# Attention with a gated expert layer, 16 batches on one core: when the projection matrix and the value bias are prepared, which engine subtracts the input's low half, and how a pair's second unit is scored

## The chip, the cores and the metric

One core of one Trainium2 chip. The metric is the device time of one launch in microseconds (us). The kernel before took 1359.69 us, the median of three runs (1359.64 to 1359.70).

## The reference

For each of 16 batches of 512 tokens with 128 features (all float32):

```
xn  = layernorm(x)                                  # no gain, no bias
q,k,v = xn @ Wq^T + bq, xn @ Wk^T + bk, xn @ Wv^T + bv   # 16 heads of 64
att = softmax(mask(q k^T / 8)) / 8                  # causal
a   = reshape(att @ v) @ proj                       # proj: 1024 x 128
g   = one-hot(argmax) * softmax(l2norm(xn Wp^T + bp) @ l2norm(sim) * exp(min(temp, ...)))   # 4 experts
f   = xn @ W^T + sum_e g_e * (xn Wd_e^T) Wu_e^T     # ranks 1, 2, 4, 8
out = x + a + f
```

The attention result is reshaped from (head, token, 64) without a transposition: each head fills 32 of the 512 rows.

## The kernel before, in words

**Precision.** Large products are made of three matmuls on fp32r operands, each operand being a high part (a rounded copy) and a low part (the rest): high by high, high by low, low by high. Where the contraction is over 64 elements only, two of the three are put on one matmul over 128 partitions: `q_parts` holds a head's high and low query halves, `k_twice` its high keys twice. A second matmul adds the low keys, `k_low`, whose other 64 rows are zero (L1246).

**Units and steps.** A batch is 8 pairs of heads (`NPAIR`), a pair is 4 units (`NBLK`): unit i scores 128 queries against its first 128(i+1) keys. A batch has 32 steps, one unit each (s = 4p + i). In step s the tensor engine scores unit s, both heads (`score`, L1227), transposes the probabilities of unit s-3 (`transpose`, L1248), runs the job of the step if `JOBS` has one (a q, k or v projection, the input's transposition `xt` in step 25, the router in step 1, the gated values in step 17), the value product of a pair every fourth step, and quarters of the output projection. Each engine has this order written out by hand in its own `step`, and the engines meet at semaphores only. Step numbers stand in constants at the top (`STEP_...`).

**Who does what.** For unit s the vector engine (DVE) takes the masked maximum out of PSUM (`maximum`, L934), the scalar engine (ACT) the exponentials with their sums (L693), DVE the reciprocals (L932), GpSimd (POOL) the multiplication by them (`normalise`, L601, the instruction is L608). ACT evacuates the transposed probabilities of head 0 (L704), DVE those of head 1 (L955). For a q or k job ACT makes the high half, DVE the low half, POOL pads the low keys (L568), and SyncE (SP) copies the halves into `q_parts` and `k_twice` by DMA (L438 to L448). For `xt` (step 25, `FIRST_X`) ACT makes `xt`, `xq_hi`, `xt_hi`, and DVE subtracts `xq_lo` (L823) and `xt_lo` (L839). In DVE's step the order is: maximum of head 0, maximum of head 1, `router_early` (L976), then `follow()` (reciprocals and the evacuation L955), `router_late` (L1000), jobs and statistics. In the last unit of a pair `follow()` stands between the two maxima.

**PSUM.** Two banks `scores`. A pair's first unit (i = 0) has both heads in bank 0: one matmul of `q_hi` against the low keys of both heads (L1222), then one per head (L1225). Units 1 to 3 have head h in bank h, two matmuls per head (L1243, L1246). `place` tells DVE where a head lies. Before unit 1 the tensor engine waits for both maxima of unit 0 (L1242).

**First batch.** Setup is mixed into its first steps. SP loads `projs`, the 1024 x 128 projection matrix, into a corner of `pt` (L482). POOL splits it into `proj_hi` and `proj_lo` after `normalise` of step 1 (L597, L599). DVE makes the three parts of the experts' up matrices in step 1 (`experts_up`, L900) and the value bias in step 3 (`value_bias`, L919), for which the tensor engine has made, after step 2, one transposition and eight float32 matmuls `bvt` by `projs` (L1210, L1214). They are first used in step 24 (`lora`, L1305) and by `project` (L1291).

**End.** After the last step the tensor engine makes, in this order: transposition of unit -3, values of pair -2, transposition of unit -2, the last two quarters of half the projection, transposition of unit -1, values of pair -1, and the rest.

Of the kernel before, what the change touches and what calls it, by code (L numbers as in the profile page):

```python
# [40 lines left out]
P = 128  # L41
# [164 lines left out]
def place(s, h):  # L206


    return (0, P * h) if s % NBLK == 0 else (h, 0)


def build(nc, x, Wq, bq, Wk, bk, Wv, bv, proj, W, Wp, bp, sim, temp, Wd, Wu, out):
    with ExitStack() as ctx:
# [79 lines left out]
        w_in = [pt[:, n // 2, n % 2, 0:2, :].rearrange("p a (c e) -> p (a c) e", e=E) for n in range(3)]  # L293
        projs = pt[:, 1, 1, 0:2, :].rearrange("p a (c e) -> p (a c) e", e=E)
        bv_rows = pt[:, 1, 1, 2, 0:P]
# [3 lines left out]
        z_lo = sb("z_lo", [P, 2, NPAIR, OCT, ROWS], F32R)  # L299
        y_t = sb("y_t", [P, S])  # L300


# [15 lines left out]
        proj_loaded = sem("proj_loaded")  # L318
        proj_split = sem("proj_split")
        bv_loaded = sem("bv_loaded")  # L320
        heads_marked = sem("heads_marked")
# [79 lines left out]
        def _(sp):  # L401
# [79 lines left out]
            sp.wait_ge(qk_moved[0], setup.moved(NPAIR))  # L481
            sp.dma_start(projs, proj.rearrange("(c p) e -> p c e", p=P)).then_inc(proj_loaded, 16)  # L482
            for s in MOVED_STEPS:
# [14 lines left out]
        def _(pool):  # L498
# [95 lines left out]

            def projection_parts():
                pool.wait_ge(proj_loaded, 16)
                nc.gpsimd.tensor_copy(proj_hi[:], projs).then_inc(proj_split, 1)  # L597
                pool.wait_ge(proj_split, 1)
                nc.gpsimd.tensor_tensor(proj_lo[:], projs, proj_hi[:].bitcast(F32), ALU.subtract)\  # L599
                    .then_inc(proj_split, 1)  # L600

# [8 lines left out]
            def batch(b, last):  # L610
                c = Counts(pool, b)
                for s in range(UNITS):
# [21 lines left out]
                    if b == 0 and s == 1:  # L634
                        projection_parts()
                    if s == STEP_RSTD and not last:
# [155 lines left out]
        def _(dve):  # L792
# [20 lines left out]

            def job(c, s, back=0):
                kind, n = JOBS[s]
# [4 lines left out]
                if kind == "xt":  # L820
                    dve.wait_ge(xt_ready, c.at(1, 2))
                    dve.wait_ge(xq_hi_ready, c.at(1, 2))
                    nc.vector.tensor_tensor(by_parity(xq_lo[:]), evens_first(xt[:]),  # L823
                                            by_parity(xq_hi[:].bitcast(F32)), ALU.subtract).then_inc(xq_lo_ready, 1)
                if kind in HI_KINDS:
# [35 lines left out]
            done.then_inc(xn_ready, 1)  # L861

# [17 lines left out]
            nc.vector.tensor_copy(bqk[:], jobp[0][:, 0:2 * NPAIR]).then_inc(bqk_ready, 1)  # L880
            job(before, FIRST_X)
            weights(1)
# [36 lines left out]
            def value_bias():  # L919

                dve.wait_ge(proj_split, 2)
                dve.wait_ge(bias_bank_ready, 1)
                nc.vector.tensor_copy(wut[0:GATED, :], outp[0:GATED, 2 * P:3 * P]).then_inc(small_ready, 1)
                dve.wait_ge(heads_marked, 4)
                link(nc.vector.tensor_copy(bias_hi[GATED:P, :], outp[GATED:P, 0:E]))
                link(nc.vector.scalar_tensor_tensor(
                    out=wut[GATED:P, :], in0=bias_hi[GATED:P, :].bitcast(F32), scalar=late_rows[GATED:P, 0:1],
                    in1=outp[GATED:P, 0:E], op0=ALU.mult, op1=ALU.add))

# [45 lines left out]
            def router_early(c, s):  # L975


                if s == STEP_SUMS:

                    dve.wait_ge(products_ready, c.at(1, 1))  # L980
                    nc.vector.tensor_reduce(unorm[:, 0, :], usq[:], AX_X, ALU.add).then_inc(unorm_ready, 1)
                    nc.vector.tensor_reduce(lg[:, 0, :, :], uprod[:], AX_X, ALU.add).then_inc(r_chain, 1)
                if s == STEP_LOGITS:

# [8 lines left out]
                        .then_inc(lg_ready, 1)  # L993
                if s == STEP_FIRST:

                    dve.wait_ge(r_chain, c.at(R_CHAIN, 9))
                    nc.vector.tensor_reduce(row[:, 4, :], ranked, AX_X, ALU.max).then_inc(r_chain, 1)
                    dve.wait_ge(r_chain, c.at(R_CHAIN, 10))
                    nc.vector.tensor_tensor(top, ranked, over_experts(row[:, 4, :]), ALU.is_ge).then_inc(r_chain, 1)

            def router_late(c, s):


                if s == STEP_WEIGHTS:
# [66 lines left out]
            def batch(b, first, last):  # L1071
                c = Counts(dve, b)
                for s in range(UNITS):
# [4 lines left out]
                    if first and s == 1:  # L1078
                        weights(4)
                        experts_up()  # L1080
                        weights(5)
                    if first and s == 2:
                        similar_units()
                    if first and s == 3:
                        value_bias()
# [15 lines left out]
            reciprocals(c, -1)  # L1101
            evacuate_pt(c, -3)
            low_z(c, -2)
            evacuate_pt(c, -2)
            evacuate_pt(c, -1)
# [6 lines left out]
        def _(pe):  # L1112
# [53 lines left out]
            weights(0)  # L1166
            pe.wait_ge(xn_ready, 1)
            for i in range(NBLK):
                done = nc.tensor.transpose(scores[0][:, P * i:P * i + P], xn[:, i, :], ident[:])
            done.then_inc(job_ready[bank_of(FIRST_X)], 1)  # L1170
# [36 lines left out]
            def value_bias():  # L1207
# [3 lines left out]
                                    up_parts[:].rearrange("p a b -> p (a b)").bitcast(F32), ident[:])  # L1211
                pe.wait_ge(proj_loaded, 16)
# [4 lines left out]
            def first_scores(c, s):  # L1217


                p = s // NBLK  # L1220
                wait(pe, sm_ready, c.head(s - 1, 0))
                nc.tensor.matmul(scores[0][:, 0:2 * P].rearrange("p (h k) -> p h k", k=P), q_hi[:, p % 2, 0:P],  # L1222
                                 k_low[:, :, p % 2, 0:P], start=True, stop=False, skip_group_check=True)
                for h in range(2):
                    nc.tensor.matmul(scores[0][:, P * h:P * h + P], q_parts[:, h, p % 2, 0:P],  # L1225
                                     k_twice[:, h, p % 2, 0:P], start=False, stop=True,
                                     skip_group_check=True).then_inc(s_ready, 1)  # L1227

            def score(c, s, first):
                i, p = s % NBLK, s // NBLK  # L1230
                if i == 0:
# [4 lines left out]
                    pe.wait_ge(low_padded, c.values(p, 1))  # L1236
                    first_scores(c, s)
# [46 lines left out]
            def project(c, o, quarter):  # L1284

                pe.wait_ge(z_ready, c.pair(OCT_PAIRS * (o + 1) - 1))
                pe.wait_ge(proj_split, 2)
                cols = OCT * ROWS * (o % NOCT)
# [30 lines left out]
            def step(c, s, first=False, last=False, tail=False):  # L1319
# [29 lines left out]
            def batch(b, first, last):  # L1349
                c = Counts(pe, b)  # L1350
                for s in range(UNITS):
                    step(c, s, first, last)
                    if first and s == 1:
                        weights(5)
                    if first and s == 2:
                        value_bias()
# [63 lines left out]
```

## Time and profile before

| | |
|---|---|
| median of 3 runs | 1359.69 us |
| the profiled execution | 1360.15 us |
| its span | 1358.4 us |
| TensorE busy (matmul) | 1340.1 us, 99% of the span, 10925 matmuls |
| VectorE, ScalarE, GpSimd busy | 1102.7, 1088.4, 969.3 us |
| granted TensorE clock | 1.00 |

Busy time is the union of an engine's instructions. A matmul's record starts when it is issued and its end is modelled, so neighbouring records overlap; the distance between two starts tells how fast TensorE goes. "Idle before" is the time that the engine had nothing running before the instruction, with what ended it. L608 is line 608 of the kernel. In the timeline, instructions of one group are merged into one row with their count.

### The profile page before, as it was taken

The page shows a single profiled execution, that of the slowest core. Times are in us where ns is not written, and L with a number is a line of the kernel's source. Part 1 is how long each engine was busy: PE and PEld are TensorE (multiplying, and loading weights), DVE is VectorE, ACT ScalarE, POOL GpSimd, SP SyncE. Part 2 cuts the span into 40 slices and gives each one's busy share as a digit, 9 for nine tenths or more (in the row PEclk, how much of TensorE's full clock was granted, in tenths as well). Part 3 has the DMA queues.
Part 4 walks back from the last instruction along what each step waited for, and adds up shares of the span by engine and source line. Part 5 has one row for each costly group of instructions (what it writes and reads, how often), then busy time and mean ns, then how long its engine had stood idle before and what let it go on. Part 6 is the DMA issues. An engine that isn't in the chain of part 4 may idle for free. (4 is left out here: it accounts for less than half of the span.)

```text
span 1358.4 us, 34725 instructions
## 1 busy us (share of the span) xinstructions
PE 1340.1 (99%) x10925; PEld 1139.4 (84%) x10925; DVE 1102.7 (81%) x4015; ACT 1088.4 (80%) x3161; POOL 969.3 (71%) x1421
## 2 busy tenths in 40 slices
PE   6999999999999999999999999999999999999998
PEld 5788888888888888888888888888888888888887
DVE  7978878788787887878788787887878878788785
ACT  5888888878878887887878788788888887888785
POOL 6777776777766776767777667777677776677664
PEclk9999999999999999999999999999999999999999
DMA  5544444544445455444544444454454454445441
GB/s 138 117 102 113 116 116 97 124 113 105 118 106 129 95 118 124 103 112 114 118 102 113 117 108 111 112 122 110 100 122 114 103 122 113 118 97 120 113 102 48
DMA packets 112690, 150.87 MB, mean 111 GB/s; under 512 B 18239, under 2 KB 47230, under 8 KB 112510
## 3 DMA queue, kind: packets, MB, share of 16 engines
q1 hardware_dynamic: 111646, 148.36, 46.1%
q8 instruction: 91, 1.49, 0.5%
q14 instruction: 89, 0.73, 0.2%
q10 hardware_dynamic: 864, 0.29, 0.1%
HBM read 10.69 MB, written 4.19 MB: 11 GB/s over the span
## 5 line engine op out<-in xcount | busy, mean ns | idle before, releaser
L608 POOL TENSOR_TENSOR prob<-prob,rden 128x128 f32<-128x128 f32 (+3 forms) x1024 | 712.3, 720 | 292.8 <-DVE rden L932 286.6
L943 DVE CUSTOM_DVE_ANT_0 prob<-scores,mask 128x128 f32<-128x128 f32 (+3 forms) x1024 | 470.5, 487 | 210.7 <-issue 148.6
L693 ACT ACTIVATE prob<-prob,nmax 128x128 f32<-128x128 f32 (+3 forms) x1024 | 567.8, 560 | 14.0 <-DVE nmax L943 6.2
L1255 PE MATMUL ptp<-ident,prob 128*128 128x128 f32 x2560 | 370.0, 274 | 1.1 <-POOL prob L608 0.6
L1255 PEld LDWEIGHTS ptp<-ident,prob 128*128 128x128 f32 x2560 | 296.0, 141 | 30.2 <-issue 8.5
L1279 PE MATMUL zp<-pt,v_sb 128*64 128x64 f32 (+3 forms) x4096 | 307.7, 303 | 1.0 <-DVE z_lo L961 0.8
L704 ACT ACTIVATE pt<-ptp 128x128 f32<-128x128 f32 (+3 forms) x512 | 221.3, 432 | 105.5 <-PE ptp L1255 105.5
L1243 PE MATMUL scores<-k_twice,q_parts 128*128 128x256 f32 (+2 forms) x768 | 267.8, 356 | 3.1 <-DVE nmax L943 3.1
L1279 PEld LDWEIGHTS zp<-pt,v_sb 128*64 128x64 f32 x4096 | 221.6, 137 | 52.3 <-issue 14.8
L1246 PE MATMUL scores<-k_low,q_parts 128*128 128x256 f32 (+2 forms) x768 | 254.1, 338 | 0.0
L955 DVE COPY pt<-ptp 128x128 f32<-128x128 f32 (+3 forms) x512 | 243.0, 475 | 2.0 <-PE ptp L1255 1.3
L568 POOL CAST k_low<-k_lo 64x512 fp32r<-64x512 f32 x256 | 155.7, 608 | 73.7 <-DVE k_lo L831 63.2
L1243 PEld LDWEIGHTS scores<-k_twice,q_parts 128*128 128x128 f32 x768 | 144.0, 187 | 67.0 <-issue 42.7
L693 ACT ACTIVATION_READ_ACCUMULATOR prob<-prob,nmax 128x1 f32 x1024 | 198.3, 194 | 0.0
L682 ACT ACTIVATE z_hi<-zp 128x512 fp32r<-128x512 f32 x128 | 76.6, 598 | 133.2 <-PE zp L1279 131.5
L1246 PEld LDWEIGHTS scores<-k_low,q_parts 128*128 128x128 f32 x768 | 144.8, 188 | 15.2
L835 DVE SCALAR_TENSOR_TENSOR q_lo<-jobp,bqk,q_hi 128x512 fp32r<-128x512 f32 x128 | 95.2, 744 | 2.4 <-ACT q_hi L674 1.5
L831 DVE SCALAR_TENSOR_TENSOR k_lo<-jobp,bqk,k_hi 128x512 fp32r<-128x512 f32 x128 | 95.1, 743 | 0.5 <-ACT k_hi L671 0.5
L961 DVE TENSOR_TENSOR z_lo<-zp,z_hi 128x512 fp32r<-128x512 f32 x128 | 87.8, 686 | 2.5 <-ACT z_hi L682 2.5
L671 ACT ACTIVATE k_hi<-jobp,bqk 128x512 fp32r<-128x512 f32 x128 | 86.7, 677 | 0.5 <-PE jobp L1192 0.5
L674 ACT ACTIVATE q_hi<-jobp,bqk 128x512 fp32r<-128x512 f32 x128 | 85.8, 670 | 0.7 <-PE jobp L1182 0.7
L943 DVE DVE_READ_ACCUMULATOR2_ANT nmax<- 128x1 f32 x1024 | 85.1, 83 | 0.2
(183 smaller groups left out, 1829.7 us busy)
## 6 DMA issues: line engine op xcount, KB each, us to landing
k_twice<-k_hi SPq DMA_DIRECT2D x508, 128.0 KB, 2.3
q_parts<-q_lo SPq DMA_DIRECT2D x256, 128.0 KB, 2.5
q_parts<-q_hi SPq DMA_DIRECT2D x254, 128.0 KB, 2.3
xin<-in_L_attn_x_dram SPq DMA_DIRECT2D x16, 256.0 KB, 3.8
xres<-in_L_attn_x_dram SPq DMA_DIRECT2D x16, 256.0 KB, 3.1
out_dram<-osb SPq DMA_DIRECT2D x15, 256.0 KB, 2.6
pt<-in_L_attn_Wq_dram SPq DMA_DIRECT2D x1, 512.0 KB, 4.8
pt<-in_L_attn_Wk_dram SPq DMA_DIRECT2D x1, 512.0 KB, 6.8
```

What stands on the lines that cost most here:

```text
L568: nc.gpsimd.tensor_copy(k_low[own(h), h, n % 2, :], k_lo[own(h), :].bitcast(F32))\
L608: nc.gpsimd.tensor_tensor(part, part, scale, ALU.mult).then_inc(pn_ready, 1)
L693: nc.scalar.activation(part, part, ACT.Exp, bias=nmax[:, s % NROT, h:h + 1], scale=-1.0, accum_out=den[:, s % NROT, h:h + 1]).then_inc(p_r ...
L704: nc.scalar.activation(pt[:, p % 2, 0, 0:i + 1, P * i:P * i + P], src, ACT.Copy)\
L831: done = nc.vector.scalar_tensor_tensor(out=k_lo[:], in0=src[:], scalar=bqk[:, NPAIR + n:NPAIR + n + 1], in1=k_hi[:].bitcast(F32), op0=ALU ...
L835: done = nc.vector.scalar_tensor_tensor(out=q_lo[:, n % 2, :], in0=src[:], scalar=bqk[:, n:n + 1], in1=q_hi[:, n % 2, :].bitcast(F32), op0 ...
L943: nc.vector.tensor_tensor_reduce(out=prob[:, s % NROT, h, 0:cols], in0=scores[bank][:, first_col:first_col + cols], in1=mask[:, S - cols:S ...
L955: nc.vector.tensor_copy(pt[:, p % 2, 1, 0:i + 1, P * i:P * i + P], src).then_inc(pt_ready[1], 1)
L1243: nc.tensor.matmul(scores[h][:, 0:width(s)], q_parts[:, h, p % 2, queries], k_twice[:, h, p % 2, 0:width(s)], start=True, stop=False)
L1246: nc.tensor.matmul(scores[h][:, 0:width(s)], q_parts[:, h, p % 2, queries], k_low[:, h, p % 2, 0:width(s)], start=False, stop=True).then_i ...
L1255: done = nc.tensor.transpose(ptp[h][:, P * j:P * j + P], prob[:, s % NROT, h, P * j:P * j + P], ident[:])
L1279: done = nc.tensor.matmul(zp[DH * odd:DH * odd + DH, z0 + P // 2 * j:z0 + S // 2], v_sb[:, j, col:col + DH], seen, start=j == NBLK - 1, st ...
```

## The change

1. A pair's second unit (i = 1) is scored like the first: one bank (bank 1) holds both heads, one matmul of `q_hi` against both heads' low keys (512 columns), then one of 256 columns per head. `maximum` waits for both heads there. The waits for free banks follow: unit 1 waits for the last maximum of the unit two before it, unit 2 head 0 for unit 0, head 1 for unit 1.
2. `xt_lo` is subtracted by POOL (`low_inputs`, at the head of step 25, before `normalise`) in all batches; only the setup's own stays on DVE.
3. `proj` is loaded in two halves into `y_t` and `osb`. POOL splits them in steps 6 and 10 of the first batch, and in step 14 adds up its eight 128 x 128 chunks in three additions; the value bias is then one matmul in place of eight. The tensor engine does this after step 18, DVE `experts_up` in step 13 and `value_bias` in step 21.
4. The router's logits (step 6) come behind the reciprocals and the evacuation L955 in DVE's step (`router_late`), no longer ahead of them.
5. In the setup each normalised block of `xn` is signalled by itself, so its transposition can start.
6. At the end the tensor engine transposes unit -1 ahead of the two projection quarters, and DVE evacuates unit -2 ahead of `low_z`.

```
 def place(s, h):
-    return (0, P * h) if s % NBLK == 0 else (h, 0)
+    return (s % NBLK, width(s) * h) if s % NBLK < 2 else (h, 0)
...
+STEP_SPLIT, STEP_SUMMED, STEP_UP, STEP_BIAS_BANK, STEP_BIAS = (6, 10), 14, 13, 18, 21
...
+            def projection_parts(half):
+                chunks = slice(NBLK * half, NBLK * half + NBLK)
+                pool.wait_ge(proj_loaded, 32)
+                nc.gpsimd.tensor_copy(proj_hi[:, chunks, :], proj_in[half]).then_inc(proj_split, 1)
+                pool.wait_ge(proj_split, 2 * half + 1)
+                nc.gpsimd.tensor_tensor(proj_lo[:, chunks, :], proj_in[half], proj_hi[:, chunks, :].bitcast(F32),
+                                        ALU.subtract).then_inc(proj_split, 1)
+            def projection_sum():
+                pool.wait_ge(proj_split, 4)
+                nc.gpsimd.tensor_tensor(proj_in[0], proj_in[0], proj_in[1], ALU.add).then_inc(proj_summed, 1)
+                for n, cols in enumerate((2 * E, E)):
+                    pool.wait_ge(proj_summed, n + 1)
+                    nc.gpsimd.tensor_tensor(y_t[:, 0:cols], y_t[:, 0:cols], y_t[:, cols:2 * cols], ALU.add)\
+                        .then_inc(proj_summed, 1)
+            def low_inputs(c):
+                made = c.fixed(c.hi(FIRST_X))
+                pool.wait_ge(job_hi[bank_of(FIRST_X)], made)
+                nc.gpsimd.tensor_tensor(xt_lo[:], xt[:], xt_hi[:].bitcast(F32), ALU.subtract)\
+                    .then_inc(job_done[bank_of(FIRST_X)], 1)
...
+                    if s == FIRST_X and not last:
+                        low_inputs(c)
                     normalise(c, s)
...
-                scored, turned = c.fixed(c.head(s, 1 if s % NBLK == 0 else h)), c.fixed(c.head(s - NROT, h))
+                scored, turned = c.fixed(c.head(s, 1 if s % NBLK < 2 else h)), c.fixed(c.head(s - NROT, h))
...
-                for n in range(NPAIR):
-                    done = nc.tensor.matmul(outp[:, 0:E], bvt[:], projs[:, n, :], start=n == 0, stop=n == NPAIR - 1)
-                done.then_inc(bias_bank_ready, 1)
+                pe.wait_ge(proj_summed, 3)
+                nc.tensor.matmul(outp[:, 0:E], bvt[:], y_t[:, 0:E], start=True, stop=True).then_inc(bias_bank_ready, 1)
+            def narrow_scores(c, s):
+                i, p = s % NBLK, s // NBLK
+                cols, queries = width(s), slice(P * i, P * i + P)
+                wait(pe, sm_ready, c.head(s - 1, 0) if i == 0 else c.head(s - 2, 1))
+                nc.tensor.matmul(scores[i][:, 0:2 * cols].rearrange("p (h k) -> p h k", k=cols), q_hi[:, p % 2, queries],
+                                 k_low[:, :, p % 2, 0:cols], start=True, stop=False, skip_group_check=True)
                 for h in range(2):
+                    nc.tensor.matmul(scores[i][:, cols * h:cols * h + cols], q_parts[:, h, p % 2, queries],
+                                     k_twice[:, h, p % 2, 0:cols], start=False, stop=True,
                                      skip_group_check=True).then_inc(s_ready, 1)
...
-                    wait(pe, sm_ready, c.head(s - 1, 1 if i == 1 else h))
+                    wait(pe, sm_ready, c.head(s - 1, h) if i == 3 else c.head(s - 2 + h, 1))
...
+                if first and s == STEP_BASE:
+                    pe.wait_ge(wut_ready, 2)
...
             transpose(c, -2)
+            transpose(c, -1)
             project(c, -2, 2)
             project(c, -2, 3)
-            transpose(c, -1)
```

## Rows read from the trace of the kernel before

**Rows 1.** Source view of L1138, the input's transposition, four matmuls in each batch

```profile
L1138 PE MATMUL jobp<-ident,xn x60: 272/273/273, 82.4 to 1243.8; 128*128 128x128 f32 x60
```

**Rows 2.** Stretches: length, then busy time of PE, PEld, DVE, ACT, POOL

```profile
622.00:664.00 42.00, 42.00 (x348) 36.11 (x346) 35.38 (x131) 33.97 (x102) 30.64 (x45) 1.00 0.48 111
```

**Rows 3.** Timeline of TensorE, first batch: start, length, line, [idle before <- releaser]

```profile
9.60 1.12 PE L1161 MATMUL outp<-ident,pt 128*128 128x128 f32 x4 [0.44 <-DMA pt<-in_L_attn_Wk_dram]
...
24.62 1.95 PE L1214 MATMUL outp<-pt,bvt 128*128 128x128 f32 x16
...
32.49 0.39 PE L1243 MATMUL scores<-k_twice,q_parts 128*128 128x256 f32 x1 [2.36 <-DVE nmax L943]
```

**Rows 4.** Timeline of TensorE's weight loads at 28.4 us

```profile
28.42 0.19 PEld L1222 LDWEIGHTS scores<-k_low,q_hi 128*128 128x128 f32 x1 [0.44 <-DMA k_twice<-k_hi]
```

**Rows 5.** Timeline of VectorE, first batch

```profile
23.93 0.48 DVE L906 TENSOR_TENSOR up_parts<-small_in,up_parts 128x32 fp32r<-128x32 f32 x1
...
30.89 0.29 DVE L923 CAST wut<-outp 96x128 fp32r<-96x128 f32 x1 [1.91 <-POOL proj_lo L599]
...
31.93 0.29 DVE L943 CUSTOM_DVE_ANT_0 prob<-scores,mask 128x128 f32<-128x128 f32 x1
```

**Rows 6.** Timeline of GpSimd, first batch

```profile
27.37 1.03 POOL L597 CAST proj_hi<-pt 128x1024 fp32r<-128x1024 f32 x1
28.48 2.37 POOL L599 TENSOR_TENSOR proj_lo<-pt,proj_hi 128x1024 fp32r<-128x1024 f32 x1
30.81 1.61 POOL L608 TENSOR_TENSOR prob<-prob,rden 128x384 f32<-128x384 f32 x2
```

**Rows 7.** Timeline of TensorE: transpositions of a 128-key unit in steps 3, 7 and 27

```profile
606.93 0.38 PE L1255 MATMUL ptp<-ident,prob 128*128 128x128 f32 x2
...
616.86 0.51 PE L1255 MATMUL ptp<-ident,prob 128*128 128x128 f32 x2
...
668.29 0.48 PE L1255 MATMUL ptp<-ident,prob 128*128 128x128 f32 x2
```

**Rows 8.** Timeline of VectorE ahead of the stall in step 7

```profile
615.27 0.32 DVE L987 TENSOR_TENSOR lg<-lg,unorm 128x16 f32<-128x16 f32 x1
...
616.25 0.67 DVE L955 COPY pt<-ptp 128x512 f32<-128x512 f32 x1
```

**Rows 9.** Timeline of VectorE ahead of the stall in step 27

```profile
665.18 0.91 DVE L823 TENSOR_TENSOR xq_lo<-xt,xq_hi 128x512 fp32r<-128x512 f32 x1 [1.04 <-ACT xq_hi L668]
666.02 0.68 DVE L839 TENSOR_TENSOR xt_lo<-xt,xt_hi 128x512 fp32r<-128x512 f32 x1
...
667.65 0.67 DVE L955 COPY pt<-ptp 128x512 f32<-128x512 f32 x1
```

**Rows 10.** Timeline of ScalarE, then of GpSimd, around step 25

```profile
664.95 0.62 ACT L669 ACTIVATE xt_hi<-jobp 128x512 fp32r<-128x512 f32 x1
...
667.88 2.84 POOL L608 TENSOR_TENSOR prob<-prob,rden 128x256 f32<-128x256 f32 x4 [2.32 <-DVE rden L932]
```

**Rows 11.** Timeline of TensorE: starts of 512-column and of 256-column matmuls

```profile
606.00 0.39 PE L1243 MATMUL scores<-k_twice,q_parts 128*128 128x512 f32 x1
606.23 0.40 PE L1246 MATMUL scores<-k_low,q_parts 128*128 128x512 f32 x1
...
610.00 0.28 PE L1243 MATMUL scores<-k_twice,q_parts 128*128 128x256 f32 x1
610.12 0.28 PE L1246 MATMUL scores<-k_low,q_parts 128*128 128x256 f32 x1
```

**Rows 12.** Groups of instructions, VectorE from 100 to 1300 us: count | busy, mean | idle before

```profile
L943 DVE CUSTOM_DVE_ANT_0 prob<-scores,mask 128x384 f32<-128x384 f32 x232 | 120.1, 554 | 120.6 <-issue 110.4 <-PE scores L1246 10.2
```

**Rows 13.** Waits, 100 to 1300 us: who <- for whom: total us, times, longest

```profile
PEld scores L1243 <- DVE nmax L943: 3.8, 18, 0.3
```

**Rows 14.** Timeline of TensorE at the end

```profile
1334.10 0.39 PE L1243 MATMUL scores<-k_twice,q_parts 128*128 128x256 f32 x1 [0.77 <-DVE nmax L943]
...
1348.52 2.40 PE L1279 MATMUL zp<-pt,v_sb 128*64 128x64 f32 x32 [0.25 <-ACT pt L704]
```

More of the change, by code:

```diff
@@ L319, in build @@
         proj_split = sem("proj_split")
+        proj_summed = sem("proj_summed")
+        wut_ready = sem("wut_ready")
+        xn_block = sem("xn_block")
         bv_loaded = sem("bv_loaded")
@@ L481, in _ @@
             sp.wait_ge(qk_moved[0], setup.moved(NPAIR))
-            sp.dma_start(projs, proj.rearrange("(c p) e -> p c e", p=P)).then_inc(proj_loaded, 16)
+            for half in range(2):
+                sp.dma_start(proj_in[half], proj.rearrange("(c p) e -> p c e", p=P)[:, NBLK * half:NBLK * half + NBLK, :])\
+                    .then_inc(proj_loaded, 16)
             for s in MOVED_STEPS:
@@ L633, in batch @@
                         pad_low_keys(c, s)
-                    if b == 0 and s == 1:
-                        projection_parts()
+                    if b == 0 and s in STEP_SPLIT:
+                        projection_parts(STEP_SPLIT.index(s))
+                    if b == 0 and s == STEP_SUMMED:
+                        projection_sum()
                     if s == STEP_RSTD and not last:
@@ L812, in variances, with job @@
                 nc.vector.tensor_tensor(var_eps[:], meanvar[:, :, 1], eps[:], ALU.add).then_inc(var_ready, 1)
-            def job(c, s, back=0):
+            def job(c, s, back=0, setup=False):
                 kind, n = JOBS[s]
@@ L824, in job @@
                                             by_parity(xq_hi[:].bitcast(F32)), ALU.subtract).then_inc(xq_lo_ready, 1)
+                    if not setup:
+                        return
                 if kind in HI_KINDS:
@@ L860, in _ @@
                                                ALU.subtract, ALU.mult)
-            done.then_inc(xn_ready, 1)
+                done.then_inc(xn_block if n < NBLK - 1 else xn_ready, 1)
             links = [0]
@@ L880, in _ @@
             nc.vector.tensor_copy(bqk[:], jobp[0][:, 0:2 * NPAIR]).then_inc(bqk_ready, 1)
-            job(before, FIRST_X)
+            job(before, FIRST_X, setup=True)
             weights(1)
@@ L982, in router_early, with router_late @@
                     nc.vector.tensor_reduce(lg[:, 0, :, :], uprod[:], AX_X, ALU.add).then_inc(r_chain, 1)
+                if s == STEP_FIRST:
+                    dve.wait_ge(r_chain, c.at(R_CHAIN, 9))
+                    nc.vector.tensor_reduce(row[:, 4, :], ranked, AX_X, ALU.max).then_inc(r_chain, 1)
+                    dve.wait_ge(r_chain, c.at(R_CHAIN, 10))
+                    nc.vector.tensor_tensor(top, ranked, over_experts(row[:, 4, :]), ALU.is_ge).then_inc(r_chain, 1)
+            def router_late(c, s):
                 if s == STEP_LOGITS:
@@ L993, in router_early @@
                         .then_inc(lg_ready, 1)
[L994 to L1001, printed above, removed]
                 if s == STEP_WEIGHTS:
@@ L1083, in batch @@
                         similar_units()
-                    if first and s == 3:
+                    if first and s == STEP_UP:
+                        experts_up()
+                    if first and s == STEP_BIAS:
                         value_bias()
@@ L1166, in _ @@
             weights(0)
-            pe.wait_ge(xn_ready, 1)
             for i in range(NBLK):
+                pe.wait_ge(xn_block, min(i + 1, NBLK - 1))
+                if i == NBLK - 1:
+                    pe.wait_ge(xn_ready, 1)
                 done = nc.tensor.transpose(scores[0][:, P * i:P * i + P], xn[:, i, :], ident[:])
@@ L1211, in value_bias @@
                                     up_parts[:].rearrange("p a b -> p (a b)").bitcast(F32), ident[:])
-                pe.wait_ge(proj_loaded, 16)
-                for n in range(NPAIR):
-                    done = nc.tensor.matmul(outp[:, 0:E], bvt[:], projs[:, n, :], start=n == 0, stop=n == NPAIR - 1)
-                done.then_inc(bias_bank_ready, 1)
[L1217 to L1223, printed above, removed]
+                pe.wait_ge(proj_summed, 3)
[6 more added lines that the diff above has]
+                                 k_low[:, :, p % 2, 0:cols], start=True, stop=False, skip_group_check=True)
                 for h in range(2):
-                    nc.tensor.matmul(scores[0][:, P * h:P * h + P], q_parts[:, h, p % 2, 0:P],
-                                     k_twice[:, h, p % 2, 0:P], start=False, stop=True,
+                    nc.tensor.matmul(scores[i][:, cols * h:cols * h + cols], q_parts[:, h, p % 2, queries],
+                                     k_twice[:, h, p % 2, 0:cols], start=False, stop=True,
                                      skip_group_check=True).then_inc(s_ready, 1)
@@ L1236, in score @@
                     pe.wait_ge(low_padded, c.values(p, 1))
-                    first_scores(c, s)
+                if i < 2:
+                    narrow_scores(c, s)
                     return
@@ L1354, in batch @@
                         weights(5)
-                    if first and s == 2:
+                    if first and s == STEP_BIAS_BANK:
                         value_bias()
```

20 lines of the change are left out of this document (6 added, 14 removed).

## The prediction

> **What bounds the kernel now.** The page comes first: TensorE has something running in 99% of the span, the next engine in 81%. Then the period: the input's transposition comes once per batch, first at 82.4 us and for the fifteenth time at 1243.8 us [rows 1], so a batch takes 1161.4 / 14 = 82.96 us, and in a stretch of 42 us in mid-run TensorE is busy for all 42.00, the others for 30.6 to 35.4 [rows 2]. From about 40 us on time is TensorE's own work. But a busy row can hide a wait, since ends are modelled and overlap, so the timeline is read for places where the same work takes longer. Two recur in each batch. The two transpositions of a 128-key unit take 0.38 us in step 3, but 0.51 in step 7 and 0.48 in step 27 [rows 7]. I found the first in 14 of 15 batches after the first one, the second in all 15 batches that have an `xt` job. Both wait for the bank that DVE's evacuation L955 frees. Last come the first 40 us and the last 25, where TensorE really is idle [rows 3, 14]. The terms are made against the profiled execution (1360.15 us, span 1358.4 and 1.75 around it); the median lies 0.46 below, and I subtract the terms from the median.
>
> **Startup.** Before, DVE comes to `value_bias` in step 3 and waits 1.91 us for POOL's `proj_lo`; with its own three operations it gets to the maximum of unit 4 only at 31.93 [rows 5]. The score of unit 5 needs it, and TensorE stands still for 2.36 us [rows 3]. POOL has spent 27.37 to 30.81, 3.44 us, on the projection's parts, with `normalise` of unit 2 behind it [rows 6]. All this leaves. Score of unit 4 does not move: it waited for the copies into `k_twice`, to 28.42 [rows 4], and SP's queue of copies stays as it is (one more load, 512 KB in two pieces, issued well before). With some 0.65 us for its three matmuls, maximum 4 starts at about 29.1 instead of 31.93, 2.8 us earlier. Score of unit 5 no longer waits for it at all, only for unit 3. POOL's unit 2 stood behind POOL's own 3.44 us only; with them gone it comes up to 3.4 us earlier, and I take 3.2, to 27.6, since its reciprocals are then the next thing late. In the timeline POOL has no gap from there to unit 8, so step by step TensorE's transpositions follow it. I take 3.1 us at step 8, bounds 2.0 (the copies for unit 8 come with only part of the shift) and 3.6 (2.36 of wait and the 1.95 us of small matmuls, less what the copies hold at 28.42). TensorE must still make the value bias, after step 18, where it is the bound: one transposition and one matmul, some 0.3 us, against the 1.95 us of before [rows 3]. Net 2.8 us.
> The moved steps need cover. `experts_up` (0.7 us, its longest operation 0.48 [rows 5]) goes to step 13, `value_bias` (1.04 us, 30.89 to 31.93) to step 21, both in a unit i = 1. Ahead of the maxima of the next unit DVE idles 120.6 us in 232, or 1.04 per unit [rows 12]; that hides them, and if it were gone they would cost 0.7 and 1.0 once. POOL's halves are 1.03 / 2 + 2.37 / 2 = 1.7 us each in steps 6 and 10 [rows 6], its sums about 2.1 (2.37 / 2 for 512 columns, half and a quarter of that for 256 and 128) in step 14. They stand in front of `normalise` of a 512-key unit, which the tensor engine wants three steps later, while POOL idles 11 us of 42 [rows 2]. Step 6 falls where POOL is late anyway: up to 1.7 us there is the lower bound's reason. Unmoved is the time to the first score: a transposition per block of `xn` ends up to 0.7 us earlier, but the next work waits for Wk's load (0.44 idle, to 9.60 [rows 3]), so 0.
>
> **Step 7.** DVE runs the logits' chain from 615.27 before the evacuation at 616.25 [rows 8]; behind it now, the evacuation starts about 0.8 us earlier and its 0.13 us of stall goes. The chain (0.9 us) ends in ACT's small exponential in step 7, in front of an evacuation: it gets its input 0.7 us later than before, which is just when ACT comes to it. 14 x 0.13 = 1.8 us; 0 if ACT becomes late.
>
> **Step 27.** DVE makes `xq_lo` and then `xt_lo` (0.68), two maxima and the late evacuation at 667.65 [rows 9]. Without `xt_lo` the maxima start when the scores allow, 0.3 us earlier or more; 0.10 is needed [rows 7]. 15 x 0.10 = 1.5 us. POOL takes it over: it has the high half at 665.57, and idles 2.32 us before 667.88 [rows 10]. Its own price is not in the trace for this form; the subtraction of twice the size took 2.37, so 1.2 us, at the earliest done at 666.8, where DVE was at 666.70. TensorE's next job on that bank comes after the transpositions of 668.29 [rows 7]. Hidden; with no cover it would cost 15 x 1.2 = 18 us.
> DVE reads two SBUF tensors in L823 to 666.09 [rows 9] just as POOL would begin. The Trainium skill (SBUF — State Buffer, "SBUF: two separate sides") says that such an operation and a GpSimd one hold a common port pair exclusively. By that rule POOL would start at 666.09 and end at 667.3, still before 667.88; no run here shows it for this pair yet.
>
> **Second unit in one bank.** Per pair, four matmuls of 256 columns become one of 512 and two of 256. Starts lie 0.23 us apart at 512 columns and 0.12 at 256 [rows 11], so nearly nothing is gained: between 0 and 0.01 us per pair. Over 128 pairs I take 0.4 us, bounds 0 and 1.3. The lost waits of scores for maxima are 3.8 us in 18 cases by weight loads, much of it hidden behind running matmuls [rows 13]: 0.4 us, bounds 0 and 0.8.
> The Trainium skill (TensorEngine Tiling, "Instruction Overhead") gives each matmul some 60 cycles of overhead, an estimate of 25 ns at 2.4 GHz and 3.2 us for 128 matmuls. The rows above speak against it.
>
> **End.** In the last batch the score of unit 29 waits 0.77 us for unit 28's maxima [rows 14]; now it waits for unit 27's. All behind it follows TensorE: 0.7 us. The new order of the tail: the transposition of unit -1 waits for unit -2's evacuation, then the projection waits for `low_z`, now behind that evacuation; by my count the last values start at about 1348.55, against 1348.52 with 0.25 us of idle before it [rows 14]. So 0, bounds -0.3 and +0.3.
>
> **Sum.** 2.8 + 1.8 + 1.5 + 0.4 + 0.4 + 0.7 = 7.6 us; 1359.69 - 7.6 = 1352.1 us. Its own range by the bounds is 1350.2 to 1354.3. A difference of 0.2%, 2.7 us, is about what a measurement can tell from none.
>
> **Rivals.** *The startup gain is held back* (0.11): POOL's 1.7 us in step 6 and again in step 10 land on transpositions. For it: no gap on POOL there; against: the unit behind each has three steps of slack. About 2 us lost: 1354.1. *The two stalls stay* (0.06), because ACT's small exponential or the scores themselves hold the evacuation: 3.3 us not won, 1355.4. *Fewer matmuls are worth more* (0.05): a matmul has a fixed part that my rounded starts hide. If each of 128 were worth a fifth of its 0.12 us slot, it would be 3.1 us, 2.7 more than taken: 1349.4; this is what the cited overhead rule would do. *Slower* (0.04): `maximum` of head 0 in the second unit now waits for the matmuls of both heads, two slots of 0.12 us later. DVE has 1.04 us of idle per unit right after [rows 12]. If the unit's chain through exponential and reciprocals sets TensorE's pace, 128 x 0.23 = 29 us come on top: 1381.5. It decides from the point at which that idle falls below 0.23. That the change does not do what it says is no case here: each of its parts is an instruction in another place.
>
> **Numbers.** The forecast has 0.74. The range 1350.0 to 1355.4 takes in the first two rivals. Faster by over 0.2% (below 1357.0): all but the slower rival and what the bounds leave: 0.93; within 0.2% 0.03; slower 0.04.
>
> **What the profile after should show.** 10783 matmul records in place of 10925 (one less in each of 128 pairs, and 2 for 16 in the bias); no TensorE idle at 30 to 32 us; unit 5's score near 30 us; batch period 82.96 - 0.25 = 82.7 us; the transpositions in steps 7 and 27 at 0.38 us; POOL's idle after step 25 shorter by 1.2 us; DVE's idle before second-unit maxima larger. I am wrong if the period is above 82.85, if a new wait of TensorE for POOL stands between 35 and 60 us, or if the first score moves.

## The result, and the profile after

The changed kernel took 1351.24 us, the median of six runs (1350.67 to 1351.71), against 1359.70 us for the kernel before beside it (1359.64 to 1359.84): the ratio is 0.9937 with a 95% interval of 0.9926 to 0.9949, some 8.5 us or 0.6% faster. The forecast was 1352.1, the range 1350.0 to 1355.4. Run again later as a yardstick it took 1351.36 against 1359.40.

The page of the kernel after, part 1, and the source view of the input's transposition [rows 1]:

```profile
PE 1330.2 (99%) x10783; PEld 1131.2 (84%) x10783; DVE 1106.4 (82%) x4000; ACT 1086.5 (81%) x3161; POOL 998.3 (74%) x1441
...
L1167 PE MATMUL jobp<-ident,xn x60: 272/273/273, 80.3 to 1234.9; 128*128 128x128 f32 x60
```

The span is 1348.9 us, the count of matmuls the 10783 that were forecast. Fourteen batches now take 1234.9 - 80.3 = 1154.6 us, before 1161.4 [rows 1]: 82.47 us each in place of 82.96, where I had forecast 82.7. So 6.8 us of the span's 9.5 lie in the steady part, 2.1 ahead of it (82.4 to 80.3), 0.6 behind. The forecast had split it otherwise: 4.1 steady, 2.8 at the start, 0.7 at the end. Of the 2.1, moreover, 0.9 lie before the first score, which stands at 17.22 instead of 18.14.

Timeline of TensorE, kernel after: step 7, then step 27 [rows 7], then the second unit of step 25 [rows 11]:

```profile
611.93 0.38 PE L1287 MATMUL ptp<-ident,prob 128*128 128x128 f32 x2
...
663.04 0.41 PE L1287 MATMUL ptp<-ident,prob 128*128 128x128 f32 x2
...
656.45 0.40 PE L1253 MATMUL scores<-k_low,q_hi 128*128 128x512 f32 x1
656.68 0.40 PE L1256 MATMUL scores<-k_twice,q_parts 128*128 128x256 f32 x2
656.92 0.38 PE L1287 MATMUL ptp<-ident,prob 128*128 128x128 f32 x2
```

The stall of step 7 is gone, that of step 27 all but 0.03 us of its 0.10. The second unit takes 656.92 - 656.45 = 0.47 us from its first start to the next work, as four matmuls of 0.12 us had taken 0.48.

Timeline around step 25, VectorE, then GpSimd [rows 9, 10]:

```profile
660.03 1.10 DVE L850 TENSOR_TENSOR xq_lo<-xt,xq_hi 128x512 fp32r<-128x512 f32 x1 [0.85 <-ACT xq_hi L695]
...
661.18 0.56 DVE L971 CUSTOM_DVE_ANT_0 prob<-scores,mask 128x384 f32<-128x384 f32 x1
```

```profile
659.31 1.28 POOL L574 CAST k_low<-k_lo 64x512 fp32r<-64x512 f32 x2 [0.41 <-DVE k_lo L860]
660.67 1.60 POOL L622 TENSOR_TENSOR xt_lo<-xt,xt_hi 128x512 fp32r<-128x512 f32 x1
662.38 1.19 POOL L631 TENSOR_TENSOR prob<-prob,rden 128x256 f32<-128x256 f32 x2
```

`xt_lo` fits: GpSimd's idle of 2.32 us is used up and `normalise` of unit 25 follows within 0.11 us. But `xq_lo` has grown from 0.91 to 1.10 us and `xt_lo` takes 1.60, not 1.2. It starts while `xq_lo` still runs and ends at 662.27, 1.14 us after `xq_lo`'s end at 661.13.

Timeline of the first batch, kernel after: TensorE, then VectorE, then GpSimd [rows 3 to 6]:

```profile
17.22 0.35 PE L1253 MATMUL scores<-k_low,q_hi 128*128 128x256 f32 x1
...
27.38 0.39 PE L1253 MATMUL scores<-k_low,q_hi 128*128 128x256 f32 x1 [1.25 <-DMA k_twice<-k_hi]
28.93 0.39 PE L1253 MATMUL scores<-k_low,q_hi 128*128 128x512 f32 x1
...
36.91 0.38 PE L1253 MATMUL scores<-k_low,q_hi 128*128 128x256 f32 x1 [1.32 <-DVE nmax L971]
...
54.68 0.50 PE L1275 MATMUL scores<-k_twice,q_parts 128*128 128x512 f32 x1 [0.25 <-DVE nmax L971]
```

```profile
50.81 1.08 DVE L1052 TENSOR_TENSOR gated<-dn,lg 128x128 f32<-128x128 f32 x1
...
53.57 0.58 DVE L935 TENSOR_TENSOR up_parts<-small_in,up_parts 128x32 fp32r<-128x32 f32 x1
54.07 0.54 DVE L971 CUSTOM_DVE_ANT_0 prob<-scores,mask 128x384 f32<-128x384 f32 x1
```

```profile
38.13 0.61 POOL L604 CAST proj_hi<-y_t 128x512 fp32r<-128x512 f32 x1
38.83 1.29 POOL L606 TENSOR_TENSOR proj_lo<-y_t,proj_hi 128x512 fp32r<-128x512 f32 x1
```

Unit 5 is scored at 28.93 instead of 32.49, with no wait; the forecast was near 30. About 1.0 of these 3.6 us is not won by the missing wait: unit 4 itself stands at 27.38 instead of 28.42, the first score being earlier. And TensorE then waits in places where it had not, or less. At the score of unit 8 (36.91) the matmul's row names the maximum of unit 7, but VectorE was done with that at 35.99; the weight load beside it waited 1.76 us for the copies into `k_twice` (0.41 before). In step 15 it waits for a maximum that VectorE reaches late, having the router's gated values (one operation of 1.08 us) and the up matrices in the same step 13.

End of the kernel after, TensorE [rows 14]:

```profile
1323.77 0.48 PE L1253 MATMUL scores<-k_low,q_hi 128*128 128x512 f32 x1
1324.09 0.40 PE L1256 MATMUL scores<-k_twice,q_parts 128*128 128x256 f32 x2
1324.96 0.41 PE L1287 MATMUL ptp<-ident,prob 128*128 128x128 f32 x2 [0.48 <-ACT pt L731]
```

The 0.77 us wait before unit 29's score is gone, but 0.48 us of it comes back one piece of work later, as a wait for ScalarE's evacuation.

### The profile page after: what moved, and what is told of

It is laid out like the page before. It is cut to its first block, busy times and chain, and to the rows that moved or that the text cites. A ratio compares the mean times of both kernels' runs of the same rounds, so it can differ in the third digit from the quotient of the medians.

```text
span 1348.9 us, 34446 instructions
## 1 busy us (share of the span) xinstructions
PE 1330.2 (99%) x10783; PEld 1131.2 (84%) x10783; DVE 1106.4 (82%) x4000; ACT 1086.5 (81%) x3161; POOL 998.3 (74%) x1441
## 4 chain that ended last, share of the span: by engine, by line
PE 95%; ACT 1%; DVE 0%; issue 0%
PE zp L1311 22%; PE ptp L1287 20%; PE jobp L1157 13%; PE scores L1275 9%; PE scores L1278 7%; PE outp L1323 7%; PE jobp L1162 6%; PE scores L1256 4%; PE scores L1253 3%; PE jobp L1172 1%; PE outp L1332 1%; ACT prob L720 1%; PE jobp L1177 1%; PE jobp L1348 0%; PE jobp L1167 0%; PE outp L1337 0%
## 5 line engine op out<-in xcount | busy, mean ns | idle before, releaser
L1275 PE MATMUL scores<-k_twice,q_parts 128*128 128x384 f32 (+1 forms) x512 | 201.3, 393 | 0.8 <-DVE nmax L971 0.8
L1278 PE MATMUL scores<-k_low,q_parts 128*128 128x384 f32 (+1 forms) x512 | 186.8, 365 | 0.0
L1275 PEld LDWEIGHTS scores<-k_twice,q_parts 128*128 128x128 f32 x512 | 95.9, 187 | 55.5 <-issue 42.7
L1278 PEld LDWEIGHTS scores<-k_low,q_parts 128*128 128x128 f32 x512 | 96.4, 188 | 9.7
L1256 PEld LDWEIGHTS scores<-k_twice,q_parts 128*128 128x128 f32 x512 | 87.5, 188 | 12.4
L1256 PE MATMUL scores<-k_twice,q_parts 128*128 128x128 f32 (+1 forms) x512 | 93.2, 263 | 0.0
L1253 PE MATMUL scores<-k_low,q_hi 128*128 128x256 f32 (+1 forms) x256 | 87.3, 341 | 2.6 <-DVE nmax L971 1.3
```

The source lines that it names most:

```text
L1256: nc.tensor.matmul(scores[i][:, cols * h:cols * h + cols], q_parts[:, h, p % 2, queries], k_twice[:, h, p % 2, 0:cols], start=False, stop= ...
```

## The experiments

Medians are set against the kernel before in the same runs. Each part of the change was put alone into the kernel before, then two of them together, then parts were taken out of or moved in the changed kernel.

**The second unit alone** (`b_narrow`: `place`, `narrow_scores` and the waits)

```
-    return (0, P * h) if s % NBLK == 0 else (h, 0)
+    return (s % NBLK, width(s) * h) if s % NBLK < 2 else (h, 0)
...
-            def first_scores(c, s):
+            def narrow_scores(c, s):
```

> The kernel before with the second unit's scoring alone (one bank, one shared low-key matmul, the new waits). From the trace of the changed kernel, where each second unit's scoring and the start behind it take 11 to 13 ns less: 128 x 0.012 = 1.5 us, and 0.3 to 0.7 us at the end where unit 29 no longer waits. Theory: 1.5 to 2.5 us faster than before. Fixed-overhead rival (25 ns per matmul left out): 3.2 us and the end's part, so 3.5 to 4 us faster. Rival of the late maximum: up to 29 us slower.

1359.59 us against 1359.49, ratio 1.0003 (0.9994 to 1.0011): no gain at all; neither the theory nor either rival said so. In its trace the steps with a second unit are each about 0.01 us shorter and unit 29's wait is gone, but step 26 has grown from 1.64 to 1.83 us in every batch.

**The logits later, alone** (`b_late`)

```
+            def router_late(c, s):
...
                 if s == STEP_LOGITS:
...
-            def router_late(c, s):
...
                 if s == STEP_WEIGHTS:
```

The head of `router_late` moves up, so that it takes in the block of the logits and runs it behind `follow()`.

> The kernel before with the router's logits behind the evacuation alone. Theory: the step-7 transpositions go from 0.51 to 0.38 us in every batch after the first, 15 x 0.12 = 1.8 us faster, and nothing else moves; step 27 stays at 0.48. Rival (ScalarE's exponential becomes late): no gain, a new wait of ScalarE before its evacuation in step 7.

1358.05 against 1359.49, ratio 0.9991 (0.9982 to 1.0000); its eleven runs, 1357.84 to 1358.73, all lie below all 33 of before, 1359.16 to 1359.84. So 1.4 us. Step 7 and step 27 of this kernel, TensorE's timeline, and ScalarE in step 7:

```profile
615.68 0.38 PE L1255 MATMUL ptp<-ident,prob 128*128 128x128 f32 x2
...
667.01 0.48 PE L1255 MATMUL ptp<-ident,prob 128*128 128x128 f32 x2
```

```profile
616.00 0.21 ACT L749 ACTIVATE lg<-lg 128x16 f32<-128x16 f32 x1
616.10 0.27 ACT L704 ACTIVATE pt<-ptp 128x128 f32<-128x128 f32 x1
```

The stall of step 7 goes and that of step 27 stays. ScalarE's exponential shows no wait before it: that rival falls.

**The low half by GpSimd, alone** (`b_low`)

```
+                    if s == FIRST_X and not last:
+                        low_inputs(c)
                     normalise(c, s)
...
+                    if not setup:
+                        return
```

> The kernel before with the input's low half by GpSimd alone. Theory: steps 26 and 27 lose 0.17 us per batch, 15 x 0.17 = 2.6 us faster; step 7 stays at 0.51. GpSimd's subtraction takes 1.6 us and VectorE's xq_lo goes from 0.91 to 1.10 because both read two tensors at the same time. Rival (the scores themselves hold the evacuation, so only the 0.10 of step 27 or nothing goes): 0 to 1.5 us.

1357.30 against 1359.49, ratio 0.9984 (0.9975 to 0.9993): 2.2 us. VectorE's timeline in this kernel, step 25 to 26:

```profile
664.01 0.93 DVE L832 TENSOR_TENSOR xq_lo<-xt,xq_hi 128x512 fp32r<-128x512 f32 x1 [1.03 <-ACT xq_hi L677]
665.18 0.56 DVE L954 CUSTOM_DVE_ANT_0 prob<-scores,mask 128x384 f32<-128x384 f32 x1 [0.25 <-PE scores L1257]
```

And GpSimd's padding beside it:

```profile
663.12 1.28 POOL L568 CAST k_low<-k_lo 64x512 fp32r<-64x512 f32 x2 [0.46 <-DVE k_lo L842]
```

VectorE now waits 0.25 us for the scores of unit 26, which it had not before; steps 26 and 27 together are 0.16 us shorter. `xq_lo` is 0.93 here, as before, and ends at 664.94, 0.54 us behind the padding; so the expected lengthening does not come from `xt_lo`; what does it is seen under `b_wait`.

**The projection matrix and the value bias later, alone** (`b_value`: the loads in halves, their split and sum, and the moved steps)

```
+STEP_SPLIT, STEP_SUMMED, STEP_UP, STEP_BIAS_BANK, STEP_BIAS = (6, 10), 14, 13, 18, 21
```

> The kernel before with the later projection matrix and value bias alone. Theory: VectorE's 1.91 us wait and GpSimd's 3.4 us go, unit 5 still waits for unit 4's maxima, and about 1 us is given back in steps 11 to 20: 1.5 to 2.8 us faster, the batch period unchanged at 82.9. Rival (the first 40 us were limited by the copies into k_twice anyway): under 1 us.

1358.52 against 1359.49, ratio 0.9992 (0.9984 to 1.0001); again no overlap (1358.25 to 1358.75). 1.0 us, the upper end of the rival and under the theory. The profile shows where it goes: the distance from unit 4's score to unit 8's is 2.1 us shorter than before, to unit 16's 1.7, to the next batch's first 1.3.

**The later maximum alone** (`b_wait`)

```
-                scored, turned = c.fixed(c.head(s, 1 if s % NBLK == 0 else h)), c.fixed(c.head(s - NROT, h))
+                scored, turned = c.fixed(c.head(s, 1 if s % NBLK < 2 else h)), c.fixed(c.head(s - NROT, h))
```

> The kernel before, with one thing only: the maximum of head 0 in a second unit waits for both heads' scores (the four matmuls and the banks stay). The second unit alone was worth nothing, though its steps became 0.1 us per batch shorter, since step 26 grew from 1.64 to 1.83 us. Theory (the later maximum does it, where VectorE has no idle before unit 26): step 26 grows by 0.1 to 0.2 us, the rest of the period does not, 1.5 to 3 us slower. Rival (the later maximum costs nothing, it was the port that GpSimd's padding and xq_lo share): no change. Second rival (it costs in all eight pairs): 29 us slower.

1362.41 against 1359.74, ratio 1.0021 (1.0012 to 1.0030): 2.7 us slower by one wait. Step 26 grows from 1.64 to 1.83 and no other step changes by more than 0.02; 15 x 0.19 = 2.9 us. Its timeline in step 25, GpSimd, then VectorE:

```profile
665.61 1.28 POOL L568 CAST k_low<-k_lo 64x512 fp32r<-64x512 f32 x2 [0.41 <-DVE k_lo L831]
```

```profile
664.73 0.74 DVE L831 SCALAR_TENSOR_TENSOR k_lo<-jobp,bqk,k_hi 128x512 fp32r<-128x512 f32 x1
666.32 1.11 DVE L823 TENSOR_TENSOR xq_lo<-xt,xq_hi 128x512 fp32r<-128x512 f32 x1 [0.84 <-ACT xq_hi L668]
```

And the same operations in the kernel before, whose `xq_lo` stands in [rows 9]:

```profile
663.40 0.74 DVE L831 SCALAR_TENSOR_TENSOR k_lo<-jobp,bqk,k_hi 128x512 fp32r<-128x512 f32 x1
```

```profile
664.28 1.27 POOL L568 CAST k_low<-k_lo 64x512 fp32r<-64x512 f32 x2 [0.46 <-DVE k_lo L831]
```

TensorE's timeline in steps 26 and 27, the kernel before, then `b_wait`:

```profile
666.40 1.03 PE L1255 MATMUL ptp<-ident,prob 128*128 128x128 f32 x8
667.23 0.50 PE L1243 MATMUL scores<-k_twice,q_parts 128*128 128x512 f32 x1
```

```profile
667.54 1.03 PE L1255 MATMUL ptp<-ident,prob 128*128 128x128 f32 x8
668.56 0.50 PE L1243 MATMUL scores<-k_twice,q_parts 128*128 128x512 f32 x1
```

This joins the theory and the first rival. The late maximum shifts `k_lo` and with it GpSimd's padding by 0.2 us: counted back from the transpositions of step 26 (666.40, 667.54), `k_lo` starts 3.00 us ahead before and 2.81 here, the padding 2.12 and 1.93. `xq_lo` still starts when ScalarE allows, 1.22 us ahead in both, but ends 0.54 us behind the padding in both kernels: 665.55 to 666.09 before, 666.89 to 667.43 here. It takes 0.69 us in the setup. The 0.54 us hold in all 15 later batches before, and in 14 of 15 here. In the one left (417.11) it begins while the first of the padding's two casts still has 0.13 us to go, and takes 0.69 us; the second cast, which began meanwhile, takes 0.98 us instead of 0.60 and ends 0.48 us behind `xq_lo`. VectorE's row, then GpSimd's:

```profile
417.11 0.69 DVE L823 TENSOR_TENSOR xq_lo<-xt,xq_hi 128x512 fp32r<-128x512 f32 x1 [0.61 <-ACT xq_hi L668]
```

```profile
417.29 0.98 POOL L568 CAST k_low<-k_lo 64x512 fp32r<-64x512 f32 x1
```

So of VectorE's operation with two SBUF inputs and GpSimd's cast, the later one is held up until the other is done. What GpSimd is late, VectorE is late, up to the maximum of unit 26, for which the score of unit 27 (667.23, 668.56) waits: it follows 0.83 us behind the transpositions before, 1.02 here. The Trainium skill (SBUF — State Buffer, "SBUF: two separate sides") says of a GpSimd operation and such a one of VectorE that whichever starts first has the shared port pair for its whole instruction, and the other fully blocks. The traces agree but for a part: 0.54 of `xq_lo`'s 0.69 us are left after the padding, so some 0.15 us of it are over by then.

**The second unit and the low half together** (`b_narrow_low`, both diffs above)

> The kernel before with the second unit's scoring and the input's low half by GpSimd together. Alone they gave 0 and 2.2 us. Theory (the low half takes away just what the later maximum collides with): step 26 comes down to 1.59, the period to 82.58, and together they give 4 to 5 us. Rival (the effects add): 2.2 us.

1354.72 against 1359.74, ratio 0.9964 (0.9951 to 0.9976): 5.0 us, where the two alone give 0 and 2.2. Step 26 is 1.59 us here. The low half takes 0.68 us of VectorE's work from just the place where the later maximum and the port hold it up.

**The changed kernel without the second unit's part** (`a_nonarrow`)

```
-                if i < 2:
-                    narrow_scores(c, s)
+                    first_scores(c, s)
                     return
```

> The changed kernel with the second unit scored as before. Theory (its worth, 0.1 us per batch of matmul starts plus the end's wait, shows once the low half is out of VectorE's way): 2 to 3 us slower than the changed kernel, steps 1, 5, 9, ... 0.012 us longer. Rival (it is worth nothing at all, as it was by itself): the same time.

1354.26 against 1351.36 for the changed kernel in the same runs: 2.9 us slower (ratios to before 0.9961, 0.9950 to 0.9973, and 0.9941, 0.9928 to 0.9953). Source views of the input's transposition, without the part, then of the changed kernel beside it (`a_again`):

```profile
L1167 PE MATMUL jobp<-ident,xn x60: 272/273/273, 80.6 to 1237.8; 128*128 128x128 f32 x60
```

```profile
L1167 PE MATMUL jobp<-ident,xn x60: 272/273/273, 80.7 to 1235.7; 128*128 128x128 f32 x60
```

1157.2 against 1155.0 us for fourteen batches: 0.157 us per batch, 20 ns for each pair. Between the unit's own starts it is 11 ns (medians over the batches, 0.476 and 0.465 us). This edit also puts the waits for free banks back, and no run parts the two. The rest, some 0.5 us, is the end's wait.

**The changed kernel again** (`a_again`, no edit)

> The changed kernel unaltered, as the common yardstick on the same chip for the three beside it. All theories: 1351.2 us, within 0.3.

1351.36 us (1351.21 to 1351.50).

**Without the signal per block of `xn`** (`a_noblock`)

```
-                done.then_inc(xn_block if n < NBLK - 1 else xn_ready, 1)
+            done.then_inc(xn_ready, 1)
```

> The changed kernel without the signal per block of xn in the setup. In the prediction it was worth nothing, as the load of Wk is waited for; in the profile of the changed kernel the first score comes 0.92 us earlier and TensorE waits for no load there. Theory (the load itself came earlier in that execution, by chance): within 0.3 us of the changed kernel. Rival (the earlier transposition is what moves the first score): 0.6 to 0.9 us slower than the changed kernel, and the first score near 18.1.

1351.47 (1351.18 to 1352.05, but for one of twelve, 1366.78) against 1351.36 (ratio to before 0.9951, 0.9933 to 0.9969): worth nothing that can be told. The first score stands at 17.76 us here. With the signal it stood at 17.22 and, in `a_again`, at 17.66; without it at 18.14 in the kernel before and at 17.42 in `b_late`. So the signal does not make the difference; that the load does is likely, but no run isolates it.

**The old order at the end** (`a_oldtail`)

```
             transpose(c, -2)
-            transpose(c, -1)
             project(c, -2, 2)
             project(c, -2, 3)
+            transpose(c, -1)
...
+            low_z(c, -2)
             evacuate_pt(c, -2)
-            low_z(c, -2)
```

> The changed kernel with the old order at the end (projection quarters ahead of unit -1's transposition, low_z ahead of unit -2's evacuation). Theory: the order is worth nothing, within 0.3 us either way, as 1348.5 was reached by both counts; by the traces the new order is 0.17 us slower between unit 31's score and the end. Rival (it was made shorter): 0.3 to 1 us slower with the old order.

1351.17 us; the changed kernel had 1351.24 and 1351.36 in other runs: no difference.

**The up matrices in step 17** (`a_up17`)

```
-STEP_SPLIT, STEP_SUMMED, STEP_UP, STEP_BIAS_BANK, STEP_BIAS = (6, 10), 14, 13, 18, 21
+STEP_SPLIT, STEP_SUMMED, STEP_UP, STEP_BIAS_BANK, STEP_BIAS = (6, 10), 14, 17, 18, 21
```

> The changed kernel with the experts' up matrices in step 17 of the first batch instead of 13. In the changed kernel's trace TensorE falls back 0.65 us in steps 13 to 16 of the first batch, where VectorE has the up matrices on top of the gated parts. Theory: that comes back, 0.3 to 0.7 us faster than the changed kernel. Rival (GpSimd's halves in steps 6 and 10 are what is late): no change.

1350.50 us (1350.04 to 1351.20). `a_oldtail`, the changed kernel but for its end, took 1351.17 (1350.73 to 1351.33) beside it, so 0.7 us, though the executions overlap. The profiles say the same: from unit 4's score to unit 16's it takes 28.70 us, against 29.37 in the changed kernel and 29.25 to 29.38 in `a_again`, `a_noblock` and `a_oldtail`. TensorE's timeline, the score of unit 15:

```profile
54.54 0.40 PE L1275 MATMUL scores<-k_twice,q_parts 128*128 128x512 f32 x1
```

It follows the job of step 14 without a wait, so that wait was VectorE's, as the theory has it.

**And GpSimd's halves later** (`a_late_split`)

```
-STEP_SPLIT, STEP_SUMMED, STEP_UP, STEP_BIAS_BANK, STEP_BIAS = (6, 10), 14, 13, 18, 21
+STEP_SPLIT, STEP_SUMMED, STEP_UP, STEP_BIAS_BANK, STEP_BIAS = (10, 14), 15, 17, 18, 21
```

> The changed kernel with the experts' up matrices in step 17, GpSimd's halves in steps 10 and 14 and the sums in step 15. Step 17 alone was worth 0.7 us. Theory (the rest that is given back in the first batch comes from GpSimd's halves and the port they share with VectorE while the transpositions still wait for it): 0.3 to 0.6 us faster than with step 17 alone, 1350.0. Rival (the value bias and the copies set it): the same as with step 17 alone, 1350.5.

1350.35 us (1350.18 to 1351.26) against 1351.36 for the changed kernel beside it; ratio to before 0.9935 (0.9923 to 0.9947). It is the fastest version measured, by 1.0 us over the changed kernel. Against `a_up17` the 0.15 us is no difference in time, as the two did not run beside each other. The profiles speak for a share of GpSimd's halves: from unit 4's score to unit 16's it takes 28.38 us here and 28.70 in `a_up17`, while the four profiles named under `a_up17` lie within 0.13. With one profile of each, the 0.3 us is an indication and not shown.

## Why the prediction was right, and where its terms were not

The time came within 0.9 us of the forecast, in part by luck: the second unit's and step 27's terms were too small, the startup's was too large. (The bounds of the terms as given add up to 9.7 us in the best case, so 1350.0 and not the 1350.2 of the sum.)

- **What bounds it.** Right. TensorE's own work is the steady state, and stalls hidden in it are found by comparing like pieces.
- **Step 7**, forecast 1.8 us: 1.4 alone. Right mechanism, size near: the step goes from 2.69 to 2.56 us in mid-run, as forecast.
- **Step 27**, forecast 1.5: 2.2 alone. The mechanism is right; the term was too small because step 26 also gives back 0.04 us and step 27 0.12, where I had only counted the two transpositions. The 0.04 is the score of unit 27 waiting for unit 26's maximum, the same wait that `b_wait` lengthens.
- **Second unit in one bank.** Here the step "Starts lie 0.23 us apart at 512 columns and 0.12 at 256 [rows 11], so nearly nothing is gained" failed: forecast 0.4 us for the matmuls and 0.4 for waits, measured 15 x 0.157 = 2.4 us for both in the changed kernel. The rows were rounded to 10 ns, and the gain is 20 ns per pair, 11 of them between the unit's own starts. The rival with a fixed part of the matmul was nearer in size than the forecast, but it is not shown to be the cause: the waits were changed in the same edit, and where the other 9 ns come from stays open. The Trainium skill (TensorEngine Tiling, "Instruction Overhead") gives each matmul some 60 cycles of overhead, an estimate of 25 ns at 2.4 GHz; the traces show 11 ns for a matmul left out between the unit's starts, 20 over the whole pair.
- **The slower rival** named the true cause, the later maximum, but another path and price. It feared the unit's chain through exponential and reciprocals, in all pairs; the runs show the chain `k_lo`, padding, `xq_lo`, maximum of unit 26, in one of eight pairs, 0.19 us, 2.7 us in all (`b_wait`). I had judged the cover by the mean idle of 1.04 us before a third unit's maximum. Before unit 26's there is none. VectorE does idle 0.84 us ahead of `xq_lo`, but that cannot take up the delay, since `xq_lo`'s end is set by GpSimd's padding. Alone, this eats the whole gain of the second unit; in the change the low half's move pays it back. That this pairing decides was not foreseen.
- **Low half on GpSimd.** Hidden, as forecast, though it takes 1.60 and not 1.2 us. The forecast by the shared port, an end 1.2 us after `xq_lo`'s, came near: 1.14.
- **Startup**, forecast 2.8: 1.0 alone. The first half of the shift came about: counted from unit 4's score, unit 5's comes 2.5 us earlier, and unit 8's 2.0 (profile after) to 3.1 (`a_noblock`) against a forecast of 3.1. Weight loads wait there for the copies into `k_twice`, 1.8 us in the former and 0.6 in the latter; that was the lower bound's reason. The step that failed is the cover of the moved work: "Ahead of the maxima of the next unit DVE idles 120.6 us in 232, or 1.04 per unit [rows 12]; that hides them" is a mean of mid-run. In step 13 the router's parts stand in the same place, and at unit 16 only 1.4 us of the shift are left. About 0.7 us of what was lost comes back with the up matrices in step 17. So the first rival was right that the gain is held back, and for these 0.7 us it named the wrong engine; GpSimd's halves may have a share of 0.3 (`a_late_split`), and the rest of the loss is not explained.
- **The end**, forecast 0.7: about 0.5; part comes back as a wait for ScalarE's evacuation. The new order is worth 0, as forecast, and so is the signal per block.
- **The signs of being wrong.** The period, 82.47 us, is under 82.85, and in the profile after TensorE has no wait for GpSimd between 35 and 60 us (in `a_again` a weight load has one, of 0.6). The first score did move, by 0.9 us in that profile, but not by the change (`a_noblock`).

The parts by their own runs: 5.0 (second unit with low half) + 1.4 + 1.0 = 7.4 of the 8.0 to 8.5 us. The remaining 0.6 to 1.1 us lies in the steady part. Source views of the input's transposition, `b_late`, `b_value`, `b_narrow_low`:

```profile
L1138 PE MATMUL jobp<-ident,xn x60: 272/273/273, 81.8 to 1241.6; 128*128 128x128 f32 x60
```

```profile
L1163 PE MATMUL jobp<-ident,xn x60: 272/273/273, 80.8 to 1242.2; 128*128 128x128 f32 x60
```

```profile
L1149 PE MATMUL jobp<-ident,xn x60: 272/273/273, 82.0 to 1239.2; 128*128 128x128 f32 x60
```

Against 1161.4 us before, fourteen batches take 1.6, 0.0 and 4.2 us less, 5.8 in sum; in the changed kernel they take 6.8 less, in `a_again` 6.4. A part of it is step 7: it takes 2.71 us in `b_narrow_low` and 2.56 in the changed kernel, so the later logits give 0.14 us per batch there, and 0.12 alone. The rest is not attributed.

## What to carry to other kernels

When one engine is busy all the time, compare like pieces of its work at different steps of the period: a stall of 0.1 us per period shows there, and not in a busy share of 42.00 us in 42.00. Judge the cover of a moved or later operation at the step where it will stand, not by the mean idle of its kind; the tightest of eight places took back a whole gain. Idle time ahead of an operation is no cover if what ends that operation is another engine. And test a change that seems to be worth nothing together with one that frees the place where it loses.

## What the runs showed that I had not expected

VectorE's subtraction of two SBUF tensors stood still while GpSimd's cast ran: 0.69 us alone, 0.91 and 1.11 beside one, the latter two ending 0.54 us behind the cast. Replacing two matmuls of 256 columns by one of 512 gave 20 ns though the columns are the same, and only 11 ns of it between the unit's own starts; where the rest comes from stays open.
